# A graph network and a mixture of experts on one core: first group of layer 0 starts with chunks 4 and 5, chunks go in release order, second expert weights and the bias rows are made between the gelus

## What is computed

```python
h = x @ W_in + b_in                                   # x is layer-normalized
for l in range(4):
    msg = segment_sum((h * dinv)[cols], rows, n) * dinv       # 100000 edges
    z = relu((h + msg) @ Wl[l] + bl[l] + mean(h, axis=0) @ Wg[l] + bg[l])
    h = layernorm(z) * gamma[l] + beta[l]
x = x + h
top_w, top_i = top_k(softmax(...mean(x) @ Wr + br...), 2)
out = sum over the 2 experts e of top_w[e] * (gelu(xn @ W1[e] + b1[e]) @ W2[e] + b2[e])
x = x + layernorm(out + xn) * gamma + beta            # xn is layer-normalized x
```

## Time and profile before

| | before |
|---|---|
| median of 3 runs | 3069.02 us |
| range of the runs | 3066.07 to 3077.74 us |
| profiled execution, its own time | 3075.48 us |
| its span, first to last instruction | 3073.9 us |
| TensorE busy (share of the span) | 2949.4 us (96%) |
| VectorE, ScalarE, GpSimd busy | 1632.5, 867.0, 82.2 us |
| mean granted TensorE clock | 0.978 |
| chain that ended last | TensorE 83%, ScalarE 9%, VectorE 3%, issue 2%, DMA 1%, SP's queue 1% |

### The profile page before, as it was taken

One profiled execution on the slowest core, in us unless ns is written; L12 is line 12 of the kernel. 1 busy time (PEld: TensorE's weight loads), 2 busy tenths in 40 slices (PEclk: granted clock), 3 DMA queues, 4 the chain that ended last, 5 costly groups with the idle time before them and its releaser, 6 DMA issues.

```text
span 3073.9 us, 54694 instructions
## 1 busy us (share of the span) xinstructions
PE 2949.4 (96%) x20138; PEld 1782.3 (58%) x20138; DVE 1632.5 (53%) x4414; ACT 867.0 (28%) x1830; POOL 82.2 (3%) x169
## 2 busy tenths in 40 slices
PE   6999998999999999999999999999999999987998
PEld 4777775545555654455556455455645555465887
DVE  8999998543443423333343333333434544466776
ACT  4888887110101100001011010010100000017775
POOL 0000000000000000000000000000000000000111
PEclk9999998999999999999999999999999999998999
DMA  4332237333332132222213222222323232211000
GB/s 128 85 86 84 84 85 175 107 93 93 99 93 69 50 96 66 73 72 72 72 47 97 67 73 72 72 72 59 85 81 83 81 85 81 78 40 41 27 25 27
DMA packets 304502, 236.51 MB, mean 77 GB/s; under 512 B 35701, under 2 KB 297316, under 8 KB 304258
## 3 DMA queue, kind: packets, MB, share of 16 engines
q1 hardware_dynamic: 297298, 218.36, 25.7%
q10 hardware_dynamic: 4608, 8.39, 0.8%
q0 software_dynamic: 2352, 6.40, 0.7%
HBM read 187.38 MB, written 45.74 MB: 76 GB/s over the span
## 4 chain that ended last, share of the span: by engine, by line
PE 83%; ACT 9%; DVE 3%; issue 2%; DMA 1%; SPq 1%; DVEq 0%; POOL 0%; ACTq 0%; POOLq 0%
PE bank L1861 66%; ACT tab L1389 8%; PE bank L1771 4%; PE bank L1956 4%; PE bank L1973 4%; PE bank L1669 1%; PE bank L1689 1%; DMA region<-adjacency 1%; PE bank L1715 1%; DVE later L874 1%; DVE region L841 1%; ACT later L1415 0%; PE bank L1700 0%; PE bank L1933 0%; ACT xnb L1409 0%
## 5 line engine op out<-in xcount | busy, mean ns | idle before, releaser
L1861 PE MATMUL bank<-region,tab 128*128 128x512 fp8e4 (+4 forms) x11712 | 2120.2, 340 | 19.3 <-DMA region<-adjacency 19.3
L1861 PEld LDWEIGHTS bank<-region,tab 128*128 128x128 f16 x11712 | 1050.5, 98 | 994.0 <-DVE region L1078 11.8
L1089 DVE SCALAR_TENSOR_TENSOR region<-bank,c_back,later 128x256 f32<-128x256 f32 x196 | 94.7, 483 | 580.5 <-PE bank L1771 580.5
L1514 ACT ACTIVATE sd<-mv,eps_c 128x1 f32<-128x1 f32 x196 | 57.8, 295 | 1081.8 <-DVE mv L1096 1081.8
L1389 ACT ACTIVATE tab<-later 128x539 fp8e4<-128x539 uint8 x584 | 334.1, 675 | 1.9 <-DVE later L874 1.9
L1078 DVE SCALAR_TENSOR_TENSOR region<-bank,s_scale,region 128x512 f16<-128x512 f32 (+2 forms) x112 | 71.4, 679 | 479.3 <-ACT region L1507 479.3
L841 DVE TENSOR_SCALAR region<-iota_w,src_at 128x540 bf16<-128x540 int16 x858 | 310.8, 414 | 0.5 <-issue 0.4
L1507 ACT ACTIVATE region<-bank,s_scale 128x512 f16<-128x512 f32 (+2 forms) x112 | 64.9, 630 | 470.1 <-PE bank L1861 470.0
L1771 PE MATMUL bank<-later,region 128*128 128x256 f16 x1176 | 160.4, 273 | 2.0 <-DVE region L1078 1.7
L1460 ACT ACTIVATE tab<-region,c_write 128x256 f32 (+1 forms) x147 | 74.7, 508 | 269.4 <-DVE region L1107 269.4
L1956 PE MATMUL bank<-tab 128*128 128x384 f16 (+1 forms) x816 | 138.2, 324 | 7.5 <-DVE tab L1245 5.3
(11 more groups left out here) (236 smaller groups left out, 1999.0 us busy)
## 6 DMA issues: line engine op xcount, KB each, us to landing
region<-adjacency SPq DMA_DIRECT2D x308, 448.0 KB, 3.4
adjacency<-tab SPq DMA_DIRECT2D x11, 3136.0 KB, 13.7
region<-adjacency SPq DMA_DIRECT2D x28, 336.0 KB, 3.1
region<-adjacency SPq DMA_DIRECT2D x56, 112.0 KB, 2.0
region<-in_x POOLq DMA_DIRECT2D x48, 128.0 KB, 2.3
out<-region SPq DMA_DIRECT2D x48, 128.0 KB, 1.7
tab<-in_x SPq DMA_DIRECT2D x5, 1024.0 KB, 11.9
dstf<-in_L_ffn_W ACTq DMA_DIRECT2D x16, 256.0 KB, 2.6
```

What stands on the lines that cost most here:

```text
L1089: tile_own.done(v.scalar_tensor_tensor(out=Z, in0=bank[4][:, 0:D], scalar=c_back[:, ds(n, 1)], in1=bias[:], op0=ALU.mult, op1=ALU.add))
L1861: ins = mm(to[k][:, d0 * P:d1 * P], tab[:, here + m, f:f + P], moving, start=q == 0 and b == 0 and moving is parts[0][0], stop=q == T - 1 ...
```

## The change

It has three parts, and two smaller moves.

1. **First group.** TensorE takes the chunks of group 0 of layer 0 in the order 4, 5, 1, 2, 3, 6, 0 (`FIRST`). SP issues the loads of chunks 4 and 5 ahead of the write of the last column; chunk 1 waits for the writes of one half of `stage` and chunk 2 for those of the other. The table tiles are made in the same order of chunks, and the first 14 of them no longer wait for the write of the last column, since they lie in the other half of `stage`. The weights of the layers are loaded from GpSimd's queue and no longer from SP's. VectorE unpacks six parts of the last column and ScalarE six; the squares and maxima (L890 to L892) stand ahead of the last mask; the first scales are made before the flag is written, and the scales of layers 1 to 3 after the table tiles. `BOUND_M` goes from 30 to 29.
2. **Order of chunks.** `chunk_order` starts from the order of group 0 and, for each group up to g, moves the group's own chunks to the end. Chunks are thus used in the order in which the group before released them.
3. **Experts.** b1 of the chosen experts is copied by VectorE out of `b1_all` (already in memory), and its two DMAs are gone. ScalarE scales the rows of the second group before the parts of W1. The parts of W2 and the b2 rows are made between the gelus of the first group.

```diff
-BOUND_M, MEAN_M, CONTEXT_M = 30, 31, 36
+ENDING = 6
+OPENING = (1, 2, 3, 4, 5, 6, 0)
+FIRST = (4, 5, 1, 2, 3, 6, 0)
+BOUND_M, MEAN_M, CONTEXT_M = 29, 31, 36
...
-        def chunk_order(g):
-            mine = sorted(set((STARTS[g] + d) // SEVEN for d in range(WIDTHS[g])))
-            return [c for c in range(T // SEVEN) if c not in mine] + mine
+        def chunk_order(g, begin=OPENING):
+            order = list(begin)
+            for k in range(1, g + 1):
+                mine = sorted(set((STARTS[k] + d) // SEVEN for d in range(WIDTHS[k])))
+                order = [c for c in order if c not in mine] + mine
+            return order
...
+            sp.wait_ge(a_written[0], 16 * (MLOOP + 1))
+            sp.wait_ge(a_written[1], 16 * MLOOP)
+            sp.wait_ge(hot_used, T * WIN)
+            for c in FIRST[:2]:
+                load(0, 0, 0, GROUP, c)
+            sp.wait_ge(last_staged, ENDING)
             write(0, T - 1, 0, 1)
-            sp.wait_ge(a_written[0], 16 * (MLOOP + 2))
-            sp.wait_ge(a_written[1], 16 * (MLOOP + 2))
...
-                for c in chunk_order(0):
+                sp.sem_inc(weights_asked, 1)
+                sp.wait_ge(a_written[1], 16 * (MLOOP + 2))
+                load(0, 0, 0, GROUP, FIRST[2])
+                sp.wait_ge(a_written[0], 16 * (MLOOP + 2))
+                load(0, 0, 0, GROUP, FIRST[3])
+                own_blocks()
+                for c in FIRST[4:]:
                     load(0, 0, 0, GROUP, c)
-                    if c == chunk_order(0)[1]:
-                        own_blocks()
-                        layer_weights()
...
-                sp.dma_start(b1_s[:, a, :], b1[ds(e, 1), :].rearrange("o (p c) -> (o p) c", c=FC)).then_inc(w1_in[a], 16)
...
+            pool.wait_ge(weights_asked, 1)
+            nc.gpsimd.dma_start(Wl_s, Wl.rearrange("l (k p) f -> p l k f", p=P)).then_inc(wl_in, 16)
+            nc.gpsimd.dma_start(Wg_s, Wg.rearrange("l (k p) f -> p (l k) f", p=P)).then_inc(wl_in, 16)
+            nc.gpsimd.dma_start(bg_s, bg.rearrange("(o l) f -> o l f", o=1).to_broadcast([P, LAYERS, D])).then_inc(wl_in, 16)
+            nc.gpsimd.dma_start(b1_all[:], b1.rearrange("e (p c) -> p e c", c=FC)).then_inc(b1_in, 16)
...
+            scales(own, 2)
             dve.wait_ge(bad_sum, 1)
             v.tensor_scalar(flag[:], bank[4][0:1, 0:1], float(NE), None, ALU.not_equal).then_inc(flag_set, 1)
...
-            act.wait_ge(a_written[0], 16 * (MLOOP + 2))
+            act.wait_ge(a_written[0], 16 * (MLOOP + 1))
             act.wait_ge(a_written[1], 16 * (MLOOP + 2))
             act.wait_ge(scales_set, 1)
...
-            with act.Fori(1, T // SEVEN) as i:
+            with act.Fori(4, 6) as i:
                 for k in range(SEVEN):
                     first_high(i * SEVEN + k)
-            for k in range(SEVEN):
-                first_high(k)
+            act.wait_ge(a_written[0], 16 * (MLOOP + 2))
+            with act.Fori(1, 4) as i:
+                for k in range(SEVEN):
+                    first_high(i * SEVEN + k)
...
+                v.tensor_copy(b1_s[:, a, :].unsqueeze(1), b1_all[:, ds(e, 1), :])
...
             xf_high(SUP - 1)
+            for t in range(SUP, 2 * SUP):
+                xf(t)
             for e in range(TOP):
                 w1_high_part(e)
-            for t in range(SUP, 2 * SUP):
-                xf(t)
...
-                if i == 0:
-                    for e in range(TOP):
-                        w2_high_part(e)
+                    if i == 0 and f in W2_AT:
+                        w2_high_part(W2_AT.index(f))
```

168 lines of the change are left out of this document (95 added, 73 removed).

## The result

| | before | after |
|---|---|---|
| median (5 runs each, the same chip) | 3072.61 us | 3052.21 us |
| range of the runs | 3066.07 to 3077.74 | 3050.95 to 3053.5 |
| ratio after to before | | 0.9932 (0.9921 to 0.9943) |
| profiled execution, its own time | 3075.48 us | 3052.21 us |
| its span | 3073.9 us | 3050.6 us |

The kernel is 0.7% faster. Forecast were 3038.7 us, a gain of 30.3 us, and a range of 3031 to 3051. Between the two profiled executions the gain is 23.3 us, and the median lies 1.2 us above the range. The direction was right and the size was not. Of the 13.5 us between forecast and median, 7.0 are the change's (30.3 forecast, 23.3 in the traces). Another 3.6 come from the median of before, which was 3069.0 over three runs and is 3072.6 over five.

What follows compares the result with a forecast made beforehand. TensorE, busy 96% of the span, was taken to bound the kernel. Gains of 10.5 + 14.3 + 5.5 = 30.3 us gave 3045.2 from the profiled 3075.5, or 3038.7 us on the median's scale, range 3031 to 3051.

Steps and rivals of the forecast that it cites:

- What bounds the kernel: Whole kernel: TensorE is busy 96% of the span, so the change wins only where TensorE is idle or slow.
- Part 1, the start, 5.6 us: Start of layer 0's first group: an earlier table chain and early chunk loads move the first aggregation matmul from 518.1 to 512.5.
- The landing times: First group's loads: chunk 4 lands near 511, chunk 5 near 513, the last column's write near 517.
- The 3.42 us wait and its 1.7 us of low clock: First group, before 536.12: wait goes because four weight loads leave SP's queue, and 1.7 us of low clock with it.
- The wait before the sum over the weight maxima: First group, source tile 29: maxima end at 539.6, TensorE arrives at 539.5; no slack, 0.2 us charged.
- The rival of late weights: First group: GpSimd's weight loads land late and VectorE, then TensorE, wait; 8 us late gives 3047, chance 0.07.
- Part 2, 14.3 us: Border of groups 1 and 2 in each layer: new chunk order saves 10.8 us of waiting and 3.5 of low clock.
- Part 3, 5.5 us: Expert stage: W2 parts and b2 rows fill idle time between gelus; first down product starts at 2797.5, not 2803.00.
- Its sign: Expert stage, what would show the gain: first down product 4 to 6 us nearer to the first up.
- The rival "part 1 gives little": Start of first group: chunk 4 behind the write or flag no earlier; 518 becomes 516, total 3044, chance 0.15.
- The lower gain of the range, 20.7 us: Whole kernel, low end: 4 + 3.4 + 10.8 + 2.5 us if clocks give nothing back, 3048 us.
- The time of a weight load on GpSimd's queue: First group: 1 MB weight takes between 2.3 and 18 us to land; short side taken, nothing charged.

Runs made afterwards that it cites:

- held_write: Changed kernel with the last column's write and the layer weights issued only once two table tiles are made; 3050.32 us, ratio 0.9932.
- late_loads: Changed kernel with the loads of chunks 4 and 5 issued behind the flag's branch, so after the last column's write; 3046.74 us, ratio 0.9921.
- weights_sp: Changed kernel with the four weight loads back on SP's queue, behind the diagonal blocks and ahead of the last three chunks; 3050.18 us, ratio 0.9935.
- after_again: Changed kernel measured once more with no edit; 3050.64 us, ratio 0.993.
- late_again: Repeat of the changed kernel with chunks 4 and 5 loaded behind the flag; 3046.65 us, ratio 0.9925.
- experts_only: Kernel before with only the expert changes: b1 copied, second group's rows scaled first, W2 parts and b2 rows between gelus; 3066.75 us, ratio 0.9985.

## Why the prediction was wrong, point by point

- **What bounds the kernel: right.** TensorE's idle and slow stretches were the places where it was won.
- **Part 1, the start, 5.6 us: wrong, −0.4 measured; this is the step that failed.** 512.5 was forecast and 518.53 came, 6.0 us later. By rows: the flag was written at 510.53, not 509.3 (1.2 us), since the last masks began at 502.04 where they had begun at 500.71, and all behind them with them. ScalarE's first tile followed 2.60 us behind it, not 1.3 (1.3 us): the read of the flag took 1.24 us where ScalarE's read took 0.47 before, which is 0.8 of it, and the rest is what ScalarE does between that read and its first tile, which the forecast left out. From the first low part's end (514.45) to TensorE's start it took 4.08 us, where 0.2 was allowed (3.9 us); the sum had no term for program that is not there yet. And 0.4 was won between the first high and the first low part. The prediction took "reading it costs 1.28 us" from a row in which the DMA engines were nearly idle, and used it for a moment in which its own plan had put a write of 784 KB. It asked of that write only who waits for its landing, not what else goes through the same engines. Held_write and late_loads show what stands in its place: with the write held back, or issued 4.3 us before the flag, the flag leads to the first matmul in 5.2 and 5.4 us and not in 8.0.
- **The landing times were nearly right.** Chunk 4 landed near 511.9 (forecast 511), chunk 5 near 513.3 (513), the last write 519.1 (517). The timely arrival of chunks 4 and 5 was worth nothing, because table and program were later.
- **The 3.42 us wait and its 1.7 us of low clock: right in size, wrong in cause, so by luck.** Group 0 took 5.3 us less, 5.1 were forecast. The prediction credited the weights' move off SP's queue; weights_sp has them on SP again and has no wait.
- **The wait before the sum over the weight maxima (0.2 us): not there.** The maxima ended at 544.3, and TensorE, itself 6 us later than forecast, took them at 545.88. The rival of late weights fell: the last of the three landed near 528.3 (514.68 + 13.6).
- **Part 2, 14.3 us: right.** 14.5 in the trace, 13.4 as the only change. Groups 1 to 2 take 17.12 us in layers 0 and 1, where 17.1 was named, and no wait for a chunk appeared at another border.
- **Part 3, 5.5 us: the total was met by luck.** The 5.5 us were forecast for the first down product alone, which came 3.9 us nearer to the end of the layers; the other 1.6 are its own faster clock, which the prediction held as an extra. Its sign, a first down product 4 to 6 us nearer to the first up, was missed: 22.92 us became 19.64, 3.3 nearer. The walk of VectorE's order was right. VectorE made the second low part of W2 from 2776.38 to 2777.66 and a gelu's low part right behind it, in the order that had been walked, and the first down product (2779.65) waited for neither. What was left out is TensorE's own work ahead of it: the up products of the second group waited 2.59 us for their rows and then took 4.80 us for 3.12.
- **Not in the sum: 1.7 us lost in the last down product**, 24 matmuls at the low clock. The prediction allowed the clock to give back what was gained in a start, not to take something at the end.
- **The sum.** 30.3 − 6.0 (start) − 1.7 (end) + 0.7 (group 0, order and rounding) = 23.3 us. The rival "part 1 gives little" had the right place and a chance of 0.15, but with "518 becomes 516" it still gave the start 2 us. Of its reasons, chunk 4 was not late, and the degrees started at 506.95 for 505.6, which is the 1.2 us above and not the other 4.8. The lower gain of the range, 20.7 us, still had 4 us of the start in it; by the medians it was 20.4. Set off from 3072.6 and not from 3069.0, the range would have ended 3.6 us higher, above the measured time; the failed step is the same.
- **The time of a weight load on GpSimd's queue.** The Trainium skill (DMA: Bandwidth & Descriptors, "Anatomy of one DMA — SWDGE (gpsimd) path") gave an estimate of 4.4 us for a weight of 1 MB. Measured from issue to landing were 9.2 us (Wl) and 11.6 us (Wg), where the DMA share was 1.1 to 1.6 (511 to 519). The measurement decides; the sum did not hang on it.

GpSimd's rows for these loads:

```profile
512.67 1.12 POOL L726 DMA_DIRECT2D region<-in_L_gnn_Wl  x1 [504.01 <-SPq L618]
513.79 0.91 POOL L727 DMA_DIRECT2D later<-in_L_gnn_Wg  x1
```

**A version that beats both kernels:** late_loads, 3046.7 us in both measurements, against 3050.6 of the changed kernel beside the first of them. From the trace of after_again to that of late_again (the fastest of its five runs, 2.0 us under their median) the span is 5.8 us shorter: 2.2 lie at the start, 2.1 between the last product and the first down product, 1.6 in the last down product (2.78 us for 4.40). In the second of these the first 18 up products take 4.37 us for 5.62 and those of the second group 4.45 for 4.80, so 1.6 of its 2.1 us are clock, as is the last. Only the first is explained by the edit; the other two came in both profiles of the late version and in none of the changed kernel, and why was not tried. The held write and the late loads were not joined.

## What to carry to other kernels

Where all engines branch on a value and their next program is not yet loaded, treat that program as a transfer that may need the DMA engines at that moment: issue large writes in small pieces well before the branch (4 us here) or only behind it. Before a load is moved ahead of a write on the same queue, read how long the issue itself will hold the queue (7.37 us here), because it delays the write as well. And measure the gain of an early load alone: here reordering by release gave 12 to 13 of the 20 to 21 us, and the early loads cost 2.2 us at the start that late_loads gets back.

## What the runs showed of the hardware

- **Reading the flag was slower shortly behind the issue of a write in small pieces.** The same read by the engines' sequencers took 0.31 to 0.49 us in most profiles and 0.64 to 1.24 us in the six where the last column's write (49 x 128 rows of 128 bytes) had been issued less than 3 us before. In the changed kernel:

```profile
L538 SPq TENSOR_LOAD <-flag x1: 1231/1231/1231, 510.7 to 510.7; - x1
L538 PEldq TENSOR_LOAD <-flag x1: 1162/1162/1162, 510.7 to 510.7; - x1
```

  and in held_write, with the two early loads in flight but not the write:

```profile
L538 SPq TENSOR_LOAD <-flag x1: 474/474/474, 509.9 to 509.9; - x1
L538 PEldq TENSOR_LOAD <-flag x1: 313/313/313, 509.9 to 509.9; - x1
```

- **A wait for program shows as "issue"**, or is put down to an engine that was long done (VectorE's 4.07 us "for ScalarE"). In the traces the first of the three packets of the instruction queues stands 1.9 to 2.3 us behind the flag in five profiles, 2.8 in late_again, and 4.5 to 5.0 us behind it in the five profiles with 7.6 to 8.0 us. That they are code behind the branch is inferred: in the seven profiles where TensorE waits for "issue" it starts 2.5 to 2.8 us after the last of them. Which engine a packet serves the traces do not say, and what in the path is slow, the read of the program, its queue or a port, stays open.
- **The clock in the last product** (2.78 us or 4.3 to 4.45 for the same 24 matmuls) changes from kernel to kernel though the 250 us ahead of it are the same to 0.1 us (0.35 longer in experts_only alone). It is worth 1.6 us, and no edit here was aimed at it.
